# An attention kernel on one core: the last row of an image without GpSimd, later reach products, layer norm means two chunks ahead

## The reference

```python
# layer 0: heads = 4, hd = 48
qkv = conv1x1(gn(x)); qkv = depthwise3x3(qkv)
q, k = l2norm(q), l2norm(k)
x = x + proj(softmax(q k^T * temperature) v)
# layer 1, per image, N = 4096 tokens, C = 192
xf = gn(x)
xn = layernorm(xf) * ln_w + ln_b
S = (xn Wq^T) (xn Wk^T)^T                    # N x N
attn = c1 * softmax(S) + c2 * relu(S)**2     # c1, c2 from w1, w2
x = x + attn (xn Wv^T) + xf
```

## Time and profile before

| | |
|---|---|
| median of 3 runs | 3390.74 us (3389.33 to 3391.31) |
| the profiled execution | 3385.89 us |
| its span, first to last instruction | 3384.1 us |
| mean granted TensorE clock | 0.972 |
| TensorE busy | 3196.7 us (94%) |
| ScalarE, VectorE, GpSimd busy | 65%, 56%, 28% |
| first mean to first scores, image 0 | 1998.08 to 2102.52 us |
| the same, image 1 | 2711.05 to 2815.99 us |
| last product with v ends | 3379.80 us |

### The profile page before, as it was taken

How to read it: one execution, slowest core, us unless ns; L and a number is a source line. 1 busy time by engine, 2 the same in 40 slices (tenths; PEclk the granted TensorE clock), 3 DMA queues, 4 the chain that set the end, 5 groups by cost and what they waited for, 6 DMA issues and landing times. The chain is left out here.

```text
span 3384.1 us, 47902 instructions
## 1 busy us (share of the span) xinstructions
PE 3196.7 (94%) x16354; PEld 1276.9 (38%) x16354; DVE 1903.8 (56%) x2461; ACT 2205.7 (65%) x2430; POOL 933.8 (28%) x485
## 2 busy tenths in 40 slices
PE   3799999999999999999998978999999788999998
PEld 1222222222223222222222224555555344555555
DVE  6551347431554524376211155888888556888886
ACT  5356556566555665565665634988888257888886
POOL 1002021020020210210200001666666214666665
PEclk8799999999999999999999989999999889999999
DMA  4412112111132021220230013677777834777777
GB/s 125 117 29 62 46 38 69 45 38 51 30 84 52 16 64 44 49 60 25 53 91 21 5 48 86 125 143 143 144 144 144 147 93 99 143 143 144 143 143 136
DMA packets 685380, 286.18 MB, mean 85 GB/s; under 512 B 602416, under 2 KB 644144, under 8 KB 682608
## 3 DMA queue, kind: packets, MB, share of 16 engines
q1 hardware_dynamic: 680656, 275.92, 38.3%
q10 hardware_dynamic: 4544, 8.00, 1.2%
HBM read 85.99 MB, written 34.21 MB: 36 GB/s over the span
## 5 line engine op out<-in xcount | busy, mean ns | idle before, releaser
L495 ACT ACTIVATE prob<-ps_s,cur 128x1024 f32<-128x1024 f32 x1024 | 1085.0, 1110 | 740.0 <-PE ps_s L715 738.9
L728 PE MATMUL ps_a<-prob,vt 128*64 128x512 f32 x4096 | 993.4, 606 | 0.0
L1486 POOL TENSOR_TENSOR p_lo<-gp,p_hi 128x1024 f16<-128x1024 f32 x256 | 550.3, 2160 | 383.6 <-ACT p_hi L1623 378.5
L1766 PE MATMUL ps_s<-kst,qs 128*128 128x512 f16 x2560 | 637.9, 382 | 15.8 <-DVEq L1957 10.6
L1779 PE MATMUL ps_o<-v_hl,at_hi 128*128 128x384 f16 x2048 | 550.0, 330 | 27.2 <-DMA at_lo<-p_lo 25.3
L709 PE MATMUL ps_s<-q_a,k_a 128*128 128x512 f16 x2048 | 535.6, 384 | 5.3 <-DMA q_b<-lo 2.1
L1779 PE MATMUL ps_o<-v_hl,at_lo 128*128 128x192 f16 x2048 | 506.4, 248 | 0.0
L728 PEld LDWEIGHTS ps_a<-prob,vt 128*64 128x64 f32 x4096 | 249.2, 136 | 409.4 <-issue 408.7
L1954 DVE TENSOR_SCALAR_CACHE_REDUCE neg<-ps_s,a_mix 128x1024 f32<-128x1024 f32 x256 | 327.3, 1279 | 114.4 <-PE ps_s L1766 113.3
L709 PEld LDWEIGHTS ps_s<-q_a,k_a 128*128 128x128 f16 x2048 | 133.5, 98 | 542.2 <-ACT prob L495 470.6
L1766 PEld LDWEIGHTS ps_s<-kst,qs 128*128 128x128 f16 x2560 | 244.3, 98 | 241.5 <-issue 14.2
(11 more groups left out here) (229 smaller groups left out, 2727.5 us busy)
## 6 DMA issues: line engine op xcount, KB each, us to landing
z<-z_scratch SPq DMA_DIRECT2D x80, 384.0 KB, 3.7
sq<-rn_scratch SPq DMA_DIRECT2D x14, 768.0 KB, 10.3
qs<-q_scratch SPq DMA_DIRECT2D x64, 128.0 KB, 2.7
rden<-den_scratch SPq DMA_DIRECT2D x64, 96.0 KB, 2.2
o_scratch<-o_s SPq DMA_DIRECT2D x64, 96.0 KB, 2.0
res_scratch<-a_xg SPq DMA_DIRECT2D x4, 1536.0 KB, 7.1
q_scratch<-qst SPq DMA_DIRECT2D x32, 192.0 KB, 2.4
res<-res_scratch SPq DMA_DIRECT2D x64, 96.0 KB, 2.1
```

The costliest lines, as they stand in the source:

```text
L495: act.activation(prob[:, n % PR, :], ps_s[:, n % 2, :], ACT.Exp, bias=cur[:, slot:slot + 1], scale=1.0 / SPLIT).then_inc(exped, 1)
L728: ins = pe.matmul(ps_a[h * HALF:(h + 1) * HALF, j % 2, :], vt[:, slot, m, :], prob[:, a % PR, h * CH:(h + 1) * CH], start=(m == 0), stop=( ...
L1486: pool.tensor_tensor(p_lo[:, cols], prob[s][:, cols], p_hi[:, cols], ALU.subtract).then_inc(lo_made[c], 1)
L1766: ins = pe.matmul(ps_s[:, c % 2, h * CH:(h + 1) * CH], qs[:, s, qt, :], kst[:, ktile, cols], start=(t == 0), stop=(t == len(terms) - 1))
```

## The change

Three things change.

1. The reach products in the last head of layer 0 come 24 steps later, at block 2, step 24.
2. The layer norm's means run two chunks ahead instead of one, in two banks in turn (the second is ps_t's first), and deviations and squares with them.
3. In the last row of each image GpSimd has no work. ScalarE makes all four high halves, VectorE all four low halves, both in the order of the chunks 0, 1, 2, 3; the loads of the next image are issued at other places among ScalarE's instructions.

```diff
-                        if last and j == 2 and m == 0:
+                        if last and j == 2 and m == 24:
                             reach_weights()
...
+        mean_at = [ps_o[0:CP, 0:CH], ps_t[0:CP, 0, :]]
...
                     square_dev(0)
+                    square_dev(1)
...
-                        if i + 1 < NCH:
-                            square_dev(i + 1)
+                        if i + 2 < NCH:
+                            square_dev(i + 2)
...
-                        if c:
-                            pe.wait_ge(dev_made, NCH * b + c)
+                        if c >= 2:
+                            pe.wait_ge(dev_made, NCH * b + c - 1)
...
                     mean_of(0)
+                    mean_of(1)
                     for i in range(NCH + 1):
                         if i < NCH:
                             variance_of(i)
-                        if i + 1 < NCH:
-                            mean_of(i + 1)
+                        if i + 2 < NCH:
+                            mean_of(i + 2)
...
                     deviate(0)
+                    deviate(1)
...
-                        if i + 1 < NCH:
-                            deviate(i + 1)
+                        if i + 2 < NCH:
+                            deviate(i + 2)
```

GpSimd's part of the last row, and the last slots of ScalarE and VectorE:

```diff
-                        low(t, s, 0)
-
-                    for t in range(RB + 1):
+                        if t < RB - 1:
+                            low(t, s, 0)
+
+                    for t in range(RB):
                         slot(t, t % 2)
...
+                    def last_slot(t, s):
+
+                        exp_piece(t, s, 3)
+                        factors(t, s)
+                        square(t, s, 0)
+                        square(t, s, 1)
+                        if b + 1 < B:
+                            act.wait_ge(s_full, b * USE + USE)
+                            for c in range(NQ):
+                                act.wait_ge(p_made[c], RB * (b + 1) - 1)
+                        bring(0, True)
+                        bring(0, False)
+                        high(t, s, 0)
+                        square(t, s, 2)
+                        bring(1, True)
+                        bring(1, False)
+                        high(t, s, 1)
+                        square(t, s, 3)
+                        bring(2, True)
+                        bring(2, False)
+                        high(t, s, 2)
+                        bring(3, True)
+                        bring(3, False)
+                        high(t, s, 3)
+                        if b + 1 < B:
                             for c in range(NQ):
                                 act.wait_ge(relued[c], RB * (b + 1))
                                 act.wait_ge(exped[c], RB * (b + 1))
                             act.wait_ge(w_done, NG * (RB * (b + 1) - 1))
-                            for c in range(NQ, NCH):
-                                bring(c, True)
-                                bring(c, False)
+                        for c in range(NQ, NCH):
+                            bring(c, True)
+                            bring(c, False)
...
-                    slot(RB - 1, 1, b + 1 < B)
-                    slot(RB, 0)
+                    last_slot(RB - 1, 1)
...
+                    def last_slot(t, s, j):
+
+                        copy_output(t - 2, s)
+                        coefficients(t, s)
+                        combine(t, s, 0)
+                        combine(t, s, 1)
+                        low(t, s, 0)
+                        combine(t, s, 2)
+                        low(t, s, 1)
+                        add_output(t - 2, s, j)
+                        combine(t, s, 3)
+                        low(t, s, 2)
+                        low(t, s, 3)
```

More of the change, by code:

```diff
@@ L1631, in bring, with slot @@
                         act.dma_start(to, src[:, cols].rearrange("(t p) n -> p t n", p=CP)).then_inc(chunk_in[c], 16)
-                    def slot(t, s, last=False):
+                    def slot(t, s):
                         exp_piece(t, s, 3)
@@ L1637, in slot @@
                         square(t, s, 0)
-                        if last:
-                            act.wait_ge(s_full, b * USE + USE)
-                            for c in range(NQ):
-                                act.wait_ge(p_made[c], RB * (b + 1) - 1)
-                            bring(0, True)
-                            bring(0, False)
                         relu(t + 1, 1 - s, 0)
                         square(t, s, 3)
-                        if last:
-                            bring(1, True)
-                            bring(1, False)
                         square(t, s, 1)
@@ L1651, in slot @@
                         high(t, s, 0)
-                        if last:
-                            bring(2, True)
-                            bring(2, False)
                         square(t, s, 2)
@@ L1661, in slot @@
                         relu(t + 1, 1 - s, 3)
-                        if last:
-                            bring(3, True)
-                            bring(3, False)
+                    def last_slot(t, s):
[22 more added lines that the diff above has]
+                        if b + 1 < B:
                             for c in range(NQ):
@@ L1711, in mean_of @@
                         pe.wait_ge(g_made, 2 * CT * b + CT * (1 + c // 4))
-                        if c:
-                            pe.wait_ge(dev_made, NCH * b + c)
+                        if c >= 2:
+                            pe.wait_ge(dev_made, NCH * b + c - 1)
                         for t in range(CT):
-                            ins = pe.matmul(ps_o[0:CP, 0:CH], meanm[:, :], g[:, t, c * CH:(c + 1) * CH],
+                            ins = pe.matmul(mean_at[c % 2], meanm[:, :], g[:, t, c * CH:(c + 1) * CH],
                                             start=(t == 0), stop=(t == CT - 1))
@@ L1891, in deviate @@
                         for t in range(CT):
-                            ins = dve.tensor_tensor(g[:, t, cols], g[:, t, cols], ps_o[0:CP, 0:CH], ALU.subtract)
+                            ins = dve.tensor_tensor(g[:, t, cols], g[:, t, cols], mean_at[c % 2], ALU.subtract)
                         ins.then_inc(dev_made, 1)
@@ L2035, in _, with low @@
                         slot(2 * r + 5, 1, r + 1)
+                    def low(row, s, c):
+                        cols = slice(c * QB, (c + 1) * QB)
+                        dve.wait_ge(hi_made[c], RB * b + row + 1)
+                        dve.tensor_tensor(p_lo[:, cols], prob[s][:, cols], p_hi[:, cols], ALU.subtract).then_inc(lo_made[c], 1)
+                    def last_slot(t, s, j):
[10 more added lines that the diff above has]
+                        low(t, s, 3)
                     for t in range(RB - 2, RB + 2):
-                        slot(t, t % 2, t // 2 - 1)
+                        if t == RB - 1:
+                            last_slot(t, t % 2, t // 2 - 1)
+                        else:
+                            slot(t, t % 2, t // 2 - 1)
                         if b + 1 < B and t in (RB - 1, RB):
```

## The result

The changed kernel took 3359.89 us (median of 4 runs, 3352.82 to 3365.46), the kernel before 3390.03 us in the same comparison (4 runs, 3385.54 to 3391.31). The ratio is 0.9914, with a 95% interval of 0.9902 to 0.9926: 29 us faster, between 25 and 33. The forecast was 3360.4.

What follows compares the result with a forecast made beforehand. TensorE is busy nine tenths nearly everywhere, so only its pauses can give time back. 15.9 + 12.0 + 2.4 + 0 = 30.3 us off 3390.74 gives 3360.4 us, range 3351 to 3369.

Steps and rivals of the forecast that it cites:

- Part 1: Last head of layer 0: reach products 24 steps later meet no wait; saves 15.9 us, bounds 12.1 to 18.3.
- Part 2: Layer norm: means two chunks ahead save 6.0 us per image, 12.0 in all; bounds 2.5 to 8.0 per image.
- the ring: Layer norm from chunk 2 on: ScalarE, GpSimd and SyncE wait in turn, 10.80 us per chunk, not touched.
- the absorbed layer norm: Layer norm: SyncE sets when chunk 2 starts, 3 instead of 6 us per image; 24 us gained, 3366; chance 0.16.
- Part 3: End of image 1: SyncE issues chunk 2's low transpose 2.37 us earlier; saves 2.4 us, bounds 0 to 3.4.
- the upper bound: End of image 1: 3.4 us, if TensorE's pause of 2.95 us shortens and last products run at 2.4 GHz.
- Part 4: End of image 0: row 30's transposes get the same share; 0 us, bounds 3 lost and 6.6 gained.
- the prediction's own signs: Among the signs of being wrong: a stall at the end of image 0 that differs by over 3 us.
- the first rival: End of image 0: loads yield, row 30's transposes land 5 us earlier; 35 us gained, 3355; chance 0.14.
- the slower rival: Rows: TensorE waits for transposes in each row; slower from 0.61 us in each of 62 rows; chance 0.02.

Runs made afterwards that it cites:

- Experiment 8: The changed kernel with the reach products 4 steps on instead of 24; 3371.02 us in a single execution.
- experiment 6: The changed kernel with loads 5 to 7 of the next image held until transposes of the last row's chunks 1 to 3 have landed; 3352.85 us.
- number 9: The changed kernel with q's stores issued ahead of k's placing and loads 5 to 7 held for the last row's chunks 1 to 3; 3329.88 us.
- number 12: The changed kernel with q's stores issued ahead of k's placing and loads 5 to 7 held for the last row's chunks 0 to 2; 3331.18 us.
- experiment 7: The changed kernel with the old order of the last row and its loads at the end of image 0 alone; 3355.73 to 3361.36 us, ratio 0.9912.
- experiment 3: The kernel before with only the new last row and load places at the ends of both images; 3388.29 us, ratio 1.0004.
- 10: The changed kernel with q's stores issued ahead of k's placing and the old end of image 0; 3330.43 us, ratio 0.9832.
- 11: The changed kernel with q's stores issued ahead of k's placing; 3329.86 us, ratio 0.9845.

## Why the prediction was right, and where its reasons were not

**Part 1, 15.9 us: right in size and cause.** 15.86 in the trace, 14.9 [9.1, 20.7] for the edit alone. The products came up at 1880.4 where 1881.1 was forecast, and took 2.50 us where 2.4 was. Experiment 8 shows the split: the clock's share of about 4 us is lost at a pause of 5.69 us too.

**Part 2, 6.0 us per image: right.** 5.7 and 7.5 in the traces, 4.5 and 7.0 for the edit alone, 11.9 measured for both. The steps of image 0 came as worked out, counted from the first mean: chunk 0's high half at 16.07 us (forecast 16.42), chunk 2's at 33.34 (33.7), the ring behind it at 10.8 for two passes and 10.7 on average. In all five traces with this edit and the old order of q's stores image 1 gains 1.7 to 2.5 us more than image 0. In the change's trace a part of that is the last cast of q, which waits 8.15 us for a store before and 7.18 after, where image 0 has 7.48 in both; why is not shown. The case against the absorbed layer norm, that SyncE waits for data and not the data for it, held for the question asked, when chunk 2 starts. It was too weak as a reading of the stage: from chunk 2 on, data did wait for SyncE, because a store that was ready stood behind a placing that was not, and the order of two calls was worth 12 us per image, twice what the change brought.

**Part 3, 2.4 us: right, 3.2 in the trace** (3.5 with the last row alone), at the top of the bounds of 0 to 3.4. The term that was misread is VectorE's. The 6.74 us of the earlier trace rows are not four combines of 1.69: three take 1.27 to 1.28, and only the fourth, which overlaps a low half of GpSimd, takes 3.14.

```profile
3358.16 3.20 POOL L1486 TENSOR_TENSOR p_lo<-gp,p_hi 128x1024 f16<-128x1024 f32 x1 [3.29 <-ACT p_hi L1623]
3359.30 3.14 DVE L1990 SCALAR_TENSOR_TENSOR gp<-gp,coef,rn 128x1024 f32<-128x1024 f32 x1
```

With GpSimd idle the combines took 1.27 to 1.28 in the change too, and the low halves 1.21 to 1.23. It cost the forecast nothing, since SyncE's own issues are the bound either way: its last issue came 2.22 us earlier (forecast 2.37). What the sum left out is the rest, some 0.9 us, which came off TensorE's waits as the upper bound had it.

**Part 4, 0 us: the number held by luck, the reason failed.** A gain and a loss cancelled that it had not foreseen. By the prediction's own signs it was wrong at this place: TensorE's wait of 6.60 us for row 30's transposes is 1.92 us in the change, a difference of over 3 us.

```profile
2630.63 0.50 PE L1793 MATMUL ps_o<-v_hl,at_hi 128*128 128x384 f16 x1 [1.92 <-DMA at_lo<-p_lo]
```

The step that failed is that ScalarE's queue holds work throughout, and that the transposes then get the same share. The traffic of the two queues, the kernel before over the first 18.9 us of the stretch (ScalarE's loads are q10, SyncE's transposes q1; the columns are packets, MB, share of 16 engines):

```profile
q10 hardware_dynamic: 1248, 2.36, 60.9%
q1 hardware_dynamic: 4936, 1.23, 53.4%
```

the changed kernel over the first 14.7 us, with the first three loads sent some 4 us apart (2616.13, 2620.81, 2624.83) and not within 5 us (2638.44, 2639.49, 2643.13):

```profile
q1 hardware_dynamic: 4844, 1.21, 62.8%
q10 hardware_dynamic: 911, 1.73, 49.7%
```

and the changed kernel from 2639.9 to 2655.6, when four loads, eight transfers, have been issued within 4.2 us:

```profile
q10 hardware_dynamic: 1657, 3.13, 77.3%
q1 hardware_dynamic: 3987, 1.08, 33.7%
```

1.2 MB of transposes went through in 14.7 us instead of 18.9 with fewer loads beside them: the loads did yield, as the first rival said. The halves are not what differs: GpSimd's last low halves of row 30 are ready 1.89 us behind row 29's output transposes before (2640.97) and 1.88 after (2618.56). With everything sent at once the loads took 77.3% and the transposes 33.7%, and the kernel before has much the same split while its first three loads are under way together, from 2639.5 to 2650:

```profile
q10 hardware_dynamic: 931, 1.77, 80.3%
q1 hardware_dynamic: 1854, 0.46, 29.7%
```

In the changed kernel the loads' queue even pauses. From 2623.6 to 2624.9 it moves next to nothing, though the load of 2620.81 takes 8.0 us to land:

```profile
q1 hardware_dynamic: 885, 0.22, 82.9%
q10 hardware_dynamic: 8, 0.01, 2.2%
```

The pause is not the whole difference: on both sides of it the loads have 57.8 and 61.8% and the transposes 58.1 and 52.8% (2617.2 to 2623.6 and 2624.9 to 2630.7). By the rule of the Trainium skill, "DMA: Bandwidth & Descriptors", Arbitration, the first two pairs should have been alike, as long as the loads' queue never ran dry; they are not, and it did pause. Whether single engines ran out of work at other moments these rows do not show, so this says that the rule did not serve as a forecast here, not that the turns are otherwise.

What the rival left out is what is late next. TensorE arrives 4.7 us earlier at row 31's transposes, and loads 4 to 7 are sent 4.7 us earlier too (23.3 us behind row 29's output transposes instead of 28.0), but the low transpose of row 31's chunk 1 is not (24.2 instead of 23.6), so that it now stands in their crowd:

```profile
2640.88 1.31 SPq L1424 DMA_TRANSPOSE at_lo<-p_lo  x1
2642.29 8.17 SPq L1422 DMA_TRANSPOSE at_hi<-p_hi  x1
```

The transpose issued at 2640.88 is the one that TensorE waits for at 2655.66; it takes 14.7 us to land, and its like in the kernel before, issued at 2662.65, takes 5.0. In the six traces with the new order it takes 12.1 to 15.8 us, in the four with the old one 5.0 to 6.3. If TensorE comes 1.3 to 3 us too early, it waits, falls to the lower clock and pays 4.4 to 5.8 us in all, the whole gain. The hold of experiment 6 does not spare this transpose much: it takes 9.5 us there, 10.7 in number 9 and 16.6 in number 12, so loads 5 to 7 are not the only ones that crowd it. That the crowd is what makes it land late is read from the traces; no run changes that alone. The prediction asked what is late next in part 1 and not here.

**The rows** took 535.3 to 537.4 us in every trace but two (experiment 7's, which is of the execution told of in the last section, and 539.22 for image 1 with the layer norm alone), so the slower rival had nothing to stand on.

**The total.** The traces' sum is 33.1 us where 30.3 was forecast, and the medians' difference 30.1 (29 by the ratio); the forecast of 3360.4 met 3359.9 more closely than its terms deserve, because the changed kernel's median lies 2.2 us further above its profiled execution than the one before did. That, like part 4, is luck.

**What stays open.** Why the profiled execution is so often the fastest where the end of image 0 is new (in five of eight kernels), and whether the spread of 11 to 17 us is all made at that place: the traces show 6.5 us of it. That the new end costs more on average than the 0.8 us gain of its traces (experiment 3 hints at it, with 3.5 us of gain at the end of image 1 in the trace and none in the median, and so do the ratios of 10 and 11, though not their medians) is not settled; the intervals overlap. No trace is of the longest execution of a kernel with the new order.

## What to carry to other kernels

When a term says that work comes earlier at one place, follow it to the next thing that the same engine waits for, and price the clock with the wait: here 1.3 us of wait, close behind another of 1.9, cost 4.4. An in-order queue that serves two streams is worth reading for what stands ready behind what is not; the largest gain of this study was two calls exchanged on SyncE. Judge an edit that races transfers against compute by the spread of its runs as well as by their median: of two versions with the same median, the one whose executions lie 1.2 us apart and not 17 is the one to keep, though five executions of each give the spreads only roughly.

## What the runs showed of the hardware

- TensorE's granted clock was 0.54 over the 10 us behind a wait of 5.69 us and 0.61 over the 10 us behind one of 12.07, and 0.73 over the 10 us around one of 1.26 us that closely followed one of 1.91. Behind a wait of 1.90 us alone it stayed at 1.00.
- Combines of VectorE on 128x1024, which read two inputs, took 1.27 to 1.28 us with GpSimd idle. The one that overlapped a low half of GpSimd took 3.14 us, and that low half 3.20 instead of some 2.1.
- The shares of two DMA queues, loads beside transposes, moved with the number of loads under way, from 58% and 58% with loads sent 4 us apart to 80% and 30% with three sent within 5 us, and 77% and 34% with four. The landing of one transpose went from 5.0 to 14.7 us.
- One execution of 62, of the kernel of experiment 7, took 6650.7 us: layer 0's products with v (L728) took 1186 ns on average instead of 606, with a granted clock of 1.00 in the records, and layer 1's scores and products 1.6 to 1.8 times theirs. The kernel's other four took 3355.73 to 3361.36. It is left out above, and nothing was found that caused it.
